# The last layer of a two-layer kernel: loop unrolled, sums normalised one step later, bias put in the PSUM banks by ScalarE

## What is computed

```python
# L1 "attention": a block-masked linear map
out = jnp.einsum('bsk,nk->bsn', data, w) + bias
# L1 "ffn": a base map and a low-rank update passed through a Fourier matrix
base = jnp.einsum('bsd,od->bso', x, W_base) + b_base
decoded = jnp.einsum('bsr,eor->ebso', e0, w0) + jnp.einsum('bsr,eor->ebso', e1, w1)
return base + real_fourier_orthogonal_multiply(decoded).sum(axis=0) * SCALING
# how each is applied
x = x + _layernorm(f(_layernorm(x, axis=-1)), axis=-1)
```

## The kernel before

| engine | order in step k |
|---|---|
| TensorE | transposes k+1; matmuls k |
| ScalarE | high parts k+1; normalise rows k+2; normalise sums k |
| VectorE | row moments k+2; low parts k+1; moments of the sums k |
| GpSimd | scale and shift of rows k+2, of sums k; two additions k |

## Time and profile before

### The profile page before, as it was taken

One profiled execution on the slowest core, in us unless ns is written; L12 is line 12 of the kernel. 1 busy time (PEld: TensorE's weight loads), 2 busy tenths in 40 slices (PEclk: granted clock), 3 DMA queues, 4 the chain that ended last, 5 costly groups with the idle time before them and its releaser, 6 DMA issues.

```text
span 1244.4 us, 16669 instructions
## 1 busy us (share of the span) xinstructions
PE 1154.3 (93%) x6096; PEld 698.8 (56%) x6096; DVE 716.4 (58%) x1370; ACT 622.8 (50%) x1043; POOL 416.1 (33%) x494
## 2 busy tenths in 40 slices
PE   4689899999999999999998899999999999999995
PEld 4535434534543344344544667788788787766663
DVE  4468588688688888978842554341231232465553
ACT  4426567467748788978775444211111111234443
POOL 1336236133412162125336555211111111134554
PEclk9989999999999999999999999999999999999998
DMA  4461430400240312103221121330030131001304
GB/s 149 101 94 57 85 56 26 103 18 2 60 86 18 94 27 37 42 27 77 45 70 43 60 68 37 102 102 1 1 102 1 15 136 68 1 34 35 101 0 135
DMA packets 71695, 72.01 MB, mean 58 GB/s; under 512 B 39954, under 2 KB 45482, under 8 KB 71596
## 3 DMA queue, kind: packets, MB, share of 16 engines
q1 hardware_dynamic: 67412, 60.22, 19.2%
q0 software_dynamic: 3152, 8.63, 2.0%
q10 hardware_dynamic: 1056, 2.16, 0.5%
HBM read 51.73 MB, written 18.87 MB: 57 GB/s over the span
## 4 chain that ended last, share of the span: by engine, by line
PE 70%; POOL 9%; issue 8%; DVE 7%; ACT 3%; DMA 2%; SPq 1%; POOLq 0%; DVEq 0%; ACTq 0%
PE PO L1435 10%; PE ST L1421 9%; PE bank L1342 9%; PE f_pair L59 6%; PE f_pair L61 6%; PE f_pair L60 6%; DVE mx L1153 3%; PE f_Y L1822 3%; PE f_Y L1824 3%; PE f_Y L1823 3%; PE bank L1345 2%; PE bank L1368 2%; PE bank L1370 2%; POOL l_rstd L2002 2%; PE bank L1369 2%
## 5 line engine op out<-in xcount | busy, mean ns | idle before, releaser
L1153 DVE TENSOR_REDUCE mx<-bank 128x1 f32<-128x512 f32 (+2 forms) x576 | 364.3, 683 | 90.8 <-PE bank L1345 54.1
L1076 ACT ACTIVATE PT<-ST,lowered 128x512 f32<-128x512 f32 x576 | 355.7, 692 | 76.1 <-PE ST L1421 65.0
L1342 PE MATMUL bank<-KS,QS 125*128 125x512 bf16 (+2 forms) x896 | 208.0, 310 | 18.3 <-DVE mx L1153 9.6
L1421 PE MATMUL ST<-QS,KS 128*128 128x512 bf16 x576 | 199.7, 386 | 3.9 <-DMA QS<-mparts 1.9
L1435 PE MATMUL PO<-PT,V 128*32 128x512 f32 x1152 | 153.3, 606 | 3.6 <-POOL PT L984 3.1
L1342 PEld LDWEIGHTS bank<-KS,QS 125*128 125x128 bf16 x896 | 77.3, 98 | 125.0 <-DVE mx L1153 51.4
L984 POOL TENSOR_SCALAR_AFFINE_SELECT PT<-PT 128x512 f32<-128x512 f32 x128 | 77.7, 638 | 201.3 <-ACT PT L1076 200.9
L1748 DVE TENSOR_TENSOR f_h<-f_h,f_pair 128x512 f32<-128x512 f32 (+1 forms) x44 | 30.2, 687 | 191.6 <-ACT f_h L1693 191.5
L59 PE MATMUL f_pair<-f_xT,gw 128*128 128x512 f32 (+1 forms) x352 | 140.1, 398 | 0.0
L61 PE MATMUL f_pair<-f_xT,gw 128*128 128x512 f32 (+1 forms) x352 | 137.9, 392 | 0.0
L60 PE MATMUL f_pair<-f_xT,gw 128*128 128x512 f32 (+1 forms) x352 | 137.8, 392 | 0.0
(11 more groups left out here) (203 smaller groups left out, 1749.5 us busy)
## 6 DMA issues: line engine op xcount, KB each, us to landing
QS<-q_scratch SPq DMA_DIRECT2D x96, 128.0 KB
l_x<-x_dram SPq DMA_DIRECT2D x12, 512.0 KB, 4.2
q_scratch<-QP SPq DMA_DIRECT2D x36, 128.0 KB, 1.9
xres<-_attn_hidden_states_dram POOLq DMA_DIRECT2D x16, 256.0 KB, 3.0
x_dram<-xout POOLq DMA_DIRECT2D x16, 256.0 KB, 2.4
xin<-x_dram SPq DMA_DIRECT2D x4, 1024.0 KB, 7.2
f_xsum<-x_dram SPq DMA_DIRECT2D x4, 1024.0 KB, 6.6
x_dram<-f_xsum SPq DMA_DIRECT2D x4, 1024.0 KB, 4.7
```

What stands on the lines that cost most here:

```text
L1076: act.activation(PT[:, quad % PT_RING, n % 4, :], ST[:, n % ST_RING, :], ACT.Exp, bias=lowered[:, 0:1]).then_inc(p_done, 1)
L1153: v.tensor_reduce(mx[:, i % 2, z, h:h + m], at(u).rearrange("p (m k) -> p m k", m=m), AX.X, ALU.max).then_inc(bank_free_dve, 1)
L1342: last = pe.matmul(at(u)[:, j * w:(j + 1) * w], QS[0:ROWS1, slot, h + j, :], KS[b][0:ROWS1, k0:k0 + w], start=(j == 0 or not diag), stop=( ...
L1421: pe.matmul(ST[:, n % ST_RING, :], KS[b][0:ROWS2, kb * P:(kb + 1) * P], QS[0:ROWS2, slot, h:h + 4, :], start=True, stop=True).then_inc(st_ ...
```

## The change

The loop becomes 16 written-out steps, with no registers, and waits against constants (`layer_of`, `duo_of`, `last_use`). Beside that:

- The normalisation of the sums of step k moves into step k+1, ahead of the rows' part there, on VectorE, GpSimd and ScalarE. The addition moves with it, behind both `scale_shift` groups.
- The bias matmul, its ones and its split are gone. The bias is loaded onto all 128 partitions, and ScalarE's `put_bias` copies it into the two banks of `prod` ahead of the matmuls, all of which now accumulate.
- Rows of duos 4 to 7 have their own buffer `x_late`. Four of the eight row loads thus no longer wait for a free buffer: two are issued in the last `ffn` block, two right behind its store.
- At the end, the last step's sums are handled tile by tile, VectorE does their two additions, and each tile of 128 rows is stored by itself.
- ScalarE, no longer TensorE, waits until `ffn` has read its output banks (`y_ready`).

```diff
         def load_bias(sp):
+            sp.wait_ge(mask_ready, 1)
             for l, b in enumerate((b_attn, b_base)):
-                sp.dma_start(braw[:, l, :], b.partition_broadcast(2)).then_inc(bias_in, 16)
+                sp.dma_start(bias[:, l, :], b.partition_broadcast(P)).then_inc(bias_in, 16)
...
         def sync(sp):
...
-                    sp.wait_ge(sum_done, g * (2 * L_STEPS) + 2 * (DUOS + d) + 6)
-
-                    sp.dma_start(x[:, d], rows(x2_dram, (DUOS + d) * DUO)).then_inc(x_in[d], 16)
-                    sp.dma_start(rows(out_dram, here[d]), xout[:, d % 2]).then_inc(x_out[d % 2], 16)
...
+            load_rows(sp, range(3 * DUOS // 2, 2 * DUOS))
+            for k in range(STEPS - 1):
+                if layer_of(k):
+                    sp.wait_ge(sum_done, 2 * k + 2)
+                    sp.dma_start(rows(out_dram, duo_of(k) * DUO), xout[:, duo_of(k) % 2]).then_inc(x_out[duo_of(k) % 2], 16)
+            for t in range(2):
+                sp.wait_ge(sum_done, 2 * (STEPS - 1) + t + 1)
+                row = duo_of(STEPS - 1) * DUO + t * P
+                sp.dma_start(out_dram[row:row + P, :], xout[:, 1, t, :]).then_inc(x_out[1], 16)
...
         def gpsimd(pool):
-            with pool.Fori(0, GROUPS) as g:
-                for k in range(L_STEPS):
-                    scale_shift(pool, 0, g, k + 2, var_x, shift_x, 4 * k + 6)
-                    scale_shift(pool, 1, g, k, var_y, shift_y, 4 * k + 8)
...
+            for k in range(STEPS):
+                if k:
+                    sums_shift(pool, k - 1)
+                if k + 2 < STEPS:
+                    rows_shift(pool, k + 2)
+                if k:
                     for t in range(2):
...
+                        add(pool, k - 1, t)
+            for t in range(2):
+                sums_shift(pool, STEPS - 1, slice(t, t + 1))
...
         def vector(v):
...
+            for k in range(STEPS):
+                if k:
+                    sum_moments(v, k - 1)
+                if k + 2 < STEPS:
+                    row_moments(v, k + 2)
+                if k + 1 < STEPS:
+                    low_parts(v, k + 1)
             for t in range(2):
+                sum_moments(v, STEPS - 1, range(t, t + 1))
+            for t in range(2):
+                add(v, STEPS - 1, t)
...
+        def put_bias(act, k):
+
+            if last_use(k) is not None:
+                act.wait_ge(yn_ready, 2 * last_use(k) + 2)
+            for t in range(2):
+                act.activation(prod[:, k % 2, t, :], bias[:, layer_of(k), :], ACT.Copy).then_inc(b_put, 1)
...
         def scalar(act):
...
+            act.wait_ge(bias_in, 32)
+            for k in range(2):
+                put_bias(act, k)
+            for k in range(STEPS):
+                if k + 1 < STEPS:
+                    high_parts(act, k + 1)
+                if k:
                     for t in range(2):
...
+                        normalize_sums(act, k - 1, t)
+                if k + 2 < STEPS:
+                    normalize(act, k + 2)
+                if 0 < k < STEPS - 1:
+                    put_bias(act, k + 1)
...
         def tensor(pe):
...
-                    pe.wait_ge(yn_ready, g * (2 * L_STEPS) + 2 * k + 2)
...
-                        pe.matmul(prod[:, k % 2, t, :], hi(ones[:, :]), hi(bias[l][:, :]), start=False, stop=True).then_inc(y_done, 1)
...
+                for t in range(2):
+                    pe.wait_ge(xtlo, 2 * k + t + 1)
+                    pe.wait_ge(b_put, 2 * k + t + 1)
```

More of the change, by code:

```diff
@@ L1870, in sb @@
             return ctx.enter_context(nc.sbuf_tensor(name, shape, dt))
-        wa, mi, blockones, gmask, msum, on, cm, ka, kb, E, M, wT0, fourier, wb, braw, bhi, bias = parts
-        bias = [bias[:, l, :] for l in range(2)]
+        wa, mi, blockones, msum, on, cm, ka, kb, E, M, wT0, fourier, wb, bias = parts
         sb("l_pad", [P, 2, DC, HALF])
@@ L1910, in layer1 @@
         wT_lo = sem("l_wT_lo")
-        b_ready = sem("l_b_ready")
+        b_put = sem("l_b_put")
         init = sem("l_init")
[L1913 to L1916, removed]
+        x_in = [sem(f"l_x_in{d}") for d in range(2 * DUOS)]
         pool_chain = sem("l_pool_chain")
@@ new lines, in sync, with scale_shift @@
+            sp.wait_ge(x_out[1], 16 * (DUOS + 1))
+        def scale_shift(pool, which, k, var, done, tiles=slice(0, 2)):
+            n, at = tiles.stop - tiles.start, (slice(None), which, k % 2, tiles)
+            pool.wait_ge(var, 2 * k + tiles.stop)
+            pool.tensor_tensor(neg_mean[at], mom[at + (0,)], minus_one[:, 0:n], ALU.mult).then_inc(pool_chain, 1)
+            pool.tensor_tensor(rstd[at], mom[at + (1,)], half_neg[:, 0:n], ALU.pow).then_inc(pool_chain, 1)
+            p_chain[0] += 2
+            pool.wait_ge(pool_chain, p_chain[0])
+            pool.tensor_tensor(shift[at], neg_mean[at], rstd[at], ALU.mult).then_inc(done, n)
@@ L2030, in moments @@
+        def moments(v, which, k, src, var, tiles=range(2)):
             s = k % 2
-            for t in range(2):
-                v.bn_stats(stats[:, which, s, t, :], src(t)).then_inc(dve, 1)
-            v.wait_ge(dve, linked - 2)
-            v.sem_inc(waited, 1)
-            for t in range(2):
-                v.bn_aggr(mom[:, which, s, t, :], stats[:, which, s, t, :]).then_inc(dve, 1)
-            v.wait_ge(dve, linked)
-            v.tensor_scalar(mom[:, which, s, :, 1], mom[:, which, s, :, 1], EPS, None, ALU.add).then_inc(var, 1)
@@ L2040, in row_moments @@
[L2040 to L2051 removed]
+            for t in tiles:
+                v.bn_stats(stats[:, which, s, t, :], src(t)).then_inc(chain, 1)
@@ new lines, in moments, with row_moments @@
+            n_chain[0] += len(tiles)
+            v.wait_ge(chain, n_chain[0])
+            for t in tiles:
+                v.bn_aggr(mom[:, which, s, t, :], stats[:, which, s, t, :]).then_inc(chain, 1)
+            n_chain[0] += len(tiles)
+            v.wait_ge(chain, n_chain[0])
+            ts = slice(tiles[0], tiles[-1] + 1)
+            v.tensor_scalar(mom[:, which, s, ts, 1], mom[:, which, s, ts, 1], EPS, None, ALU.add).then_inc(var, len(tiles))
+        def row_moments(v, k):
+            if layer_of(k):
+                v.wait_ge(sum_done, 2 * (k - DUOS) + 2)
+            else:
+                v.wait_ge(x_in[duo_of(k)], 16)
+            if last_use(k) is not None:
+                v.wait_ge(shift_x, 2 * last_use(k) + 2)
+            moments(v, 0, k, lambda t: rows_of(k)[:, t, :], var_x)
```

202 lines of the change are left out of this document (87 added, 115 removed).

## The result

| | before | after |
|---|---|---|
| median, 4 runs each on one chip | 1247.67 us (1246.66 to 1252.21) | 1210.14 us (1208.3 to 1211.11) |
| profiled execution, span | 1244.4 us | 1206.5 us |
| first transposes of `layer1` | 1096.29 | 1094.74 |
| start of the last statistics of sums (before: of both tiles; after: of the last tile) | 1231.70 | 1199.22 |
| granted TensorE clock, mean | 0.986 | 0.989 |

The ratio is 0.9701, with a 95% interval of 0.9685 to 0.9718: 37.5 us faster, where 33 had been forecast.

The account below looks back on a forecast made before the run. Bound: a two-step loop of 16.94 us holding GpSimd's additions and the sums' normalisation. Steps of 6.71 us gain 28.0; with an end of 7.65 the span ends at 1211.4, 33.0 us gained; forecast 1215, range 1209 to 1224.

Parts of the forecast that it names:

- both bounds meet: In the new loop, the way round two steps takes 13.42 us, 6.71 a step, against TensorE's own 6.70.
- M(1) to M(14): Starts of the first 128x512 matmul of steps 1 and 14: forecast 1104.6 and 1191.8, 13 steps of 6.71 us.
- the last step: Step 15 has no transposes before it, 0.85 us less: matmuls from 1197.7, second tile's statistics at 1203.7.
- 5.97 + 5.24 + 2.21 = 13.42: Two-step loop in us: first matmul to sums' statistics, on to ScalarE's next rows, on to the matmul behind the bias copy.
- The copy: ScalarE's bias copy into PSUM, shown by no row, was taken as 0.60 us; dearest form 0.81.
- my second case: A new wait where the loop's two bounds meet, by a copy over 1 us or the lock: 1219 to 1230, chance 0.15.
- The lock between VectorE and GpSimd: VectorE's epsilon instruction held by GpSimd's additions: 0.29 us a loop, 2 us in all; by the skill's rule 9 us, 1224.
- Start: Step 0's first matmul, M(0), waits for the bias copies: 0.66 us later, at 1097.74, with M(1) at 1104.6.
- End: From the last tile's statistics to the span's end: 2.5, 0.8, 0.7, 0.15 and store 3.5, sum 7.65 us, before 12.7.
- Rival "slower than before": TensorE's clock falls in 7 or more of 16 steps, each some 6 us longer: 1255 or more, chance 0.03.
- my 1234: Rival that the loop doesn't open: only bias matmuls (7.3 us) and the end (4.9) are won, 12.2; chance 0.04.

Follow-up runs that it names:

- additions_first: The changed kernel with GpSimd's additions of step k-1 put back ahead of the rows' shift of k+2: 1240.49 us, ratio 0.9947.
- two_copies: The changed kernel with each bias copy into PSUM made twice, the second waiting for the first: 1215.34 us, ratio 0.9747.
- bias_matmul: The changed kernel, new order kept, with the bias added by a two-row matmul closing each tile instead of copies: 1226.06 us, ratio 0.9830.
- old_order_bias_matmul: The changed kernel with both the three queues' old order and the bias matmuls put back: 1237.24 us, ratio 0.9926.
- no_bias: The changed kernel with the bias left out, neither copies nor bias matmuls, so the output lacks both biases: 1209.41 us, ratio 0.9707.
- shared_rows: The changed kernel with rows of duos 4 to 7 loaded back into the buffers of 0 to 3: 1226.45 us, ratio 0.9850.
- better: The changed kernel with step 0's bias copies ahead of the last weight copy and step 14's additions on VectorE: 1211.02 us, ratio 0.9711.
- old_order: The changed kernel with VectorE, GpSimd and ScalarE queues in the old order, sums of k behind rows of k+2: 1239.61 us, ratio 0.9942.
- old_order_no_bias: The changed kernel in the old queue order with both biases left out, no copies and no bias matmul: 1227.63 us, ratio 0.9847.

## Why the prediction was right, and which terms were off

**The loop, right in structure.** Rows no longer wait for additions, and `additions_first` closes the loop again by that alone. The forecast that both bounds meet holds: TensorE's own step is 6.47 and the way round the loop 6.51, and M(1) to M(14) gives 6.52 in the mean. That the loop is level and not far below is shown by `two_copies`, where one more copy lengthens it at once. The step is just under the 6.55 to 6.9 of my forecast, and the 1210.1 us lie near the lower end of my 1209 to 1224.

**Terms mis-sized, nearly all to the safe side.** The end came 4.9 us earlier than forecast: 2.4 by the steps, 0.4 by the last step, 0.4 by the end, 0.1 at the start, and 1.55 ahead of `layer1`, which was in no term of mine and which the change does not explain. Step 6.52 for 6.71, 2.4 us over 13 steps. On TensorE, the bias matmul costs 1.16 us (`bias_matmul`), not 0.95: I left the transposes a change of shape of 0.42 behind the last matmul, and it is 0.23 (1108.40 to 1108.63). In the loop I had 5.97 + 5.24 + 2.21 = 13.42 and it is 5.88 + 5.00 + 2.15 = 13.03. Most of that is 0.24 between the sums' statistics and ScalarE's rows: VectorE takes up the rows after 1.79 instead of 1.95 (1108.83 to 1110.62), and ScalarE starts 3.21 behind that (1113.83) instead of 3.29. I carried durations over from a body with registers to one without. That the registers are the cause is argued, not shown; no run kept the loop and changed the rest. The nearest is `old_order_bias_matmul`, unrolled in the old order with bias matmuls and own buffers: a pair takes 16.70 there for 16.9, and sums' statistics to ScalarE 3.22 (1120.41 to 1123.63) for 3.29.

**The copy, right.** 0.58 us in the mean for my 0.60, and 0.09 us of waiting a pair in the mean (M(1) to M(14) is 84.80 us, and 84.19 in `no_bias`). Once, at 1135.74, M stands 0.32 later than usual behind its transposes, but 0.22 of that is there without copies too. `two_copies` shows that my second case (a copy of over 1 us) would have cost 5 us.

**The lock between VectorE and GpSimd: mechanism real, and wrongly priced, but absent here.** I read 0.29 us more in one row as the price. The runs say it is the rest of the GpSimd instruction, however long that is: in `shared_rows` the epsilon instruction starts at 1146.69, and ends at 1147.72, 0.03 behind the end of the addition beside it (1147.69). Four such instructions there take 1.02 to 1.03, and the row of before ends likewise 0.04 behind the first of its two additions (1152.60 and 1152.56). This is what the Trainium skill says of two-port VectorE instructions (SBUF — State Buffer, "Who interferes with whom"), and the traces agree to 0.04 us; that this one is of that kind, no run shows. After the change no addition reaches an epsilon instruction in a step of the loop. The distance is mostly 0.7 to 0.8, for which I had 0.8, and 0.47 at the closest: the place, not the price, decided. In `better` the same wait is seen the other way round, GpSimd behind VectorE.

**Start.** M(0) lies 1.44 behind the transposes where it was 0.79: 0.65 later, forecast 0.66. It is free, as forecast: `no_bias` and `better` give it back in the next step.

**End.** 7.28 for 7.65: from the last statistics to VectorE's last addition 3.80 (1199.22 to 1203.02) for my 3.45. The last tile's shift starts on GpSimd only at 1201.14, 0.82 behind the end of its epsilon instruction (1200.32), since the first tile's shift stands in front of it, and this began only at 1200.22, when the additions of step 14 were nearly done (1200.27). I had left GpSimd's queue out of the end. The addition took 0.69 for 0.7; from there to the end of the span 2.8 for the 3.5 that I had for the store.

**The clock.** Rival "slower than before" didn't occur, for the reason given: no idle. But I had put its danger in the wrong place. It is not in a TensorE-bound step, it is in a kernel where TensorE's step got shorter than the loop by more: `old_order`, where it idles 2.3 to 2.4 us in one piece. Had the loop not opened, the result would have been 1239 to 1240 by `old_order` and `additions_first`, and not my 1234 (whose 4.9 for the end should by my own terms have been 12.7 - 7.65 = 5.05, which moves it by 0.15 only).

**Outside the change.** 1.55 us of the 37.9 stand ahead of `layer1` and weren't followed up.

## What to carry to other kernels

Where an engine alternates between a step with a wait and one without, look for the work that stands between a result and the next step's start in another engine's queue, and put it behind what releases the next step: one exchange of two groups in GpSimd's queue was worth 30 us here (by the runs in the old order some 19 for the loop and 11 for the clock), against 0.7 for all of ScalarE's copies. Judge an edit that shortens TensorE by the loop that bounds it and by the idle that it leaves: in the old order the loop's gain of 8.5 us was lost to a lower clock, with the new order the same edit was worth 16 us. And when additions move later, ask which buffers they free, and what waits for those.

## What the runs showed of the hardware that wasn't expected

- The granted clock was 0.90 in every pair of `old_order`, with one idle of 1.9 us in the first and of 2.3 to 2.4 in the others. It stayed at 1.00 with idle of 1.38 and 0.56 us a pair (`old_order_no_bias`), or of 1.1 to 1.24 (`old_order_bias_matmul`); in before it fell behind one idle of 1.36 out of seven alike. A fall costs 1.4 us a pair. Needless matmuls in the idle gave all of it back, 10.9 us of the kernel.
- A copy of 128x512 fp32 from SBUF to PSUM takes ScalarE 0.58 us (four in a row 2.15), as much as the copy out of PSUM (0.58).
- A two-row matmul that closes a tile of twelve costs TensorE 0.58 us (1.16 for two tiles), more than two ordinary ones of 0.23. In the trace of before the way into it takes 0.33 (1103.13 to 1103.46) and the way out 0.42 (to 1103.88), for 0.23 between two of one shape.
